# A graph layer with experts on one core: tighter edge slots and a reordered SyncE list in the first stage

## The chip, the cores and the metric

The kernel runs on one core of a Trainium2 chip. The metric is the device time of one execution in microseconds (us), lower is better. TensorE multiplies, VectorE, ScalarE and GpSimd compute on tiles of 128 partitions, SyncE only issues DMA transfers. Each engine works through its own list of instructions in order and waits on semaphores.

## The reference

There are N = 3125 nodes with D = 256 features and E = 50000 edges (`src`, `dst`). The edges are sorted by `dst`, and low node numbers have far more of them (`dst` is 3125 times the square of a uniform number). Cut to what matters:

```python
x_i = x[tgt]; x_j = x[src]                          # x is layer-normalised
h = relu(concatenate([x_i, x_j - x_i]) @ W1 + b1)   # 50000 x 512
out = segment_sum(h @ W2 + b2, tgt) / (deg + 1e-8)
x = x + out
# then: layernorm, a router that takes 2 of 8 experts, each expert
# gelu(xn @ W1[e] + b1[e]) @ W2[e] + b2[e], weighed and added to x
```

## The kernel before

**Splitting the product.** `feat @ W1` is P[dst] + Q[src], where Q = xn @ W1[256:] + b1 and P = xn @ (W1[:256] - W1[256:]). The hidden sum per node is multiplied by W2 only once per node.

**The Q stage** (the first block) walks over the NT = 25 tiles of 128 nodes. For tile t, TensorE transposes the normalised x (`turn`, L739), ScalarE copies it back (L696), TensorE multiplies (`product_q`, L746), VectorE adds b1 into `q_buf[t % 4]` (`keep_q`, L505), and SyncE stores that to `q_rows` in HBM (L405). `q_buf` has four parts, so `keep_q(t)` waits until the store of tile t-4 has landed (`s_qst`). Four PSUM banks hold the products, so TensorE can be up to four tiles ahead of `keep_q`. ScalarE normalises tile t+4 (L702). VectorE takes the layernorm statistics of whole groups of tiles (`statistics(k)`, L487 and L490), at the tiles given by `STATS_AT`: the last three groups are tiles 14 to 18, 19 to 23 and 24. ScalarE's `root(k)` (L692) follows and stands in its list ahead of later normalisations.

Between these, VectorE works out where each node tile's edges lie: `count_in_rows` (after `keep_q(4)`) feeds a small TensorE product (L770, behind the product of tile 6), which `find_ends` reads; then come `add_slots`, `find_tiles`, `find_blocks` (L598 to L613), which signals `s_index`. GpSimd then runs eight indirect gathers (L461) that fetch the src and dst of every slot from two copies in HBM, `src_blocks` and `dst_blocks`, and casts them (L464, L465). `first_table` (L623 to L634) uses them on VectorE at tile `SPREAD_AT`, and TensorE transposes the result two tiles later (L774, L777).

**Edge slots.** A slot is 128 consecutive edges which are handled for one node tile. Before, slots are whole blocks of 128 edges at multiples of 128 (EB = 391 of them), and a block that holds edges of two tiles takes a slot for each. So NS = 416, rounded up to 16.

**The edge stage** (the second block) processes NS slots. For each, GpSimd issues one indirect gather of 128 rows of `q_rows`, 2 KB each, into a ring of 16 (`gath`, L979). It may run until 16 slots ahead of the `seed` (L1146) or `add_z` (L1020) that frees the ring's place. TensorE expands P (L1285 to L1289), ScalarE takes the relu (L1158), VectorE its low part (L1025), TensorE sums into the tile (L1308, L1309). P itself is made in the same stage, in 46 half products between the first 368 slots.

**After it** come a stage over the 25 node tiles (W2, residual, layernorm, router) and one over 56 expert slots.

If the edges are unsorted, or the slots do not fit, a flag `unsorted` makes the kernel run the edge stage 25 times (`n_pass`).

Of the kernel before, what the change touches and what calls it, by code (L numbers as in the profile page):

```python
# [85 lines left out]
def build(nc, x, src, dst, g_w1, g_b1, g_w2, g_b2, gamma, beta, wr, br, f_w1, f_b1, f_w2, f_b2, out):  # L86
# [7 lines left out]
    NS = ceil_div(EB + NT - 1, UNROLL) * UNROLL  # L94
    SC = ceil_div(NS + 1, P)
# [26 lines left out]
    with ctx:  # L122
# [85 lines left out]
        start_i = whole("start_i", [P, 32], I32, a_ctx)  # L208
        first_i = whole("first_i", [P, 32], I32, a_ctx)
        last_i = whole("last_i", [P, 32], I32, a_ctx)  # L210
        first_f = whole("first_f", [P, 32], F32, a_ctx)
# [3 lines left out]
        nslot = whole("nslot", [P, 32], F32, a_ctx)  # L215
        shift = whole("shift", [P, 32], F32, a_ctx)
# [4 lines left out]
        eblk_i = whole("eblk_i", [P, SC], I32, a_ctx)  # L221
# [149 lines left out]
        SUMS_AT, SPREAD_AT = 6, 18  # L371
# [3 lines left out]
        with nc.Block(no_gpsimd_drain=True) as block:  # L375

            @block.sync
            def _(sp):
# [19 lines left out]
                for k, v in ((0, src), (1, dst)):  # L398
# [12 lines left out]
            def _(pool):  # L411
# [56 lines left out]
            def _(dve):  # L468
# [72 lines left out]
                def find_ends():  # L541
# [5 lines left out]
                    then(dve.tensor_copy(start_i[:, 0:NT], start_f[:, 0:NT]))  # L547
                    then(dve.tensor_scalar(last_f[:, 0:NT], start_f[:, 1:NT + 1], -1.0, 0.0, ALU.add, ALU.max))
                    now()

                    then(dve.tensor_scalar(first_i[:, 0:NT], start_i[:, 0:NT], 7, None, ALU.arith_shift_right))
# [3 lines left out]
                    then(dve.tensor_copy(first_f[:, 0:NT], first_i[:, 0:NT]))  # L555
                    now()

                    then(dve.tensor_scalar(first_f[:, 0:NT], first_f[:, 0:NT], float(EB - 1), None, ALU.min))
                    then(dve.tensor_copy(last_f[:, 0:NT], last_i[:, 0:NT]))
                    then(dve.memset(nslot[:, :], 0.0))  # L560
                    now()
                    then(dve.tensor_tensor(last_f[:, 0:NT], last_f[:, 0:NT], first_f[:, 0:NT], ALU.subtract))
                    now()

                    then(dve.tensor_scalar(nslot[:, 1:NT], last_f[:, 0:NT - 1], 0.0, 1.0, ALU.max, ALU.add))
# [13 lines left out]
                def find_tiles():  # L579

                    then(dve.tensor_tensor(shift[:, 0:NT], first_f[:, 0:NT], base[0][:, 0:NT], ALU.subtract))
                    then(dve.tensor_tensor(too_soon[:, 0:NT], first_ok[:, 0:NT], base[0][:, 0:NT], ALU.is_gt))
                    now()
                    then(dve.tensor_reduce(soonest[:, :], too_soon[:, READY:NT], AX.X, ALU.max))
# [12 lines left out]
                def find_blocks():  # L597
                    then(dve.tensor_tensor(esort[:, :], esort[:, :], slot_no[:], ALU.add))  # L598
# [4 lines left out]
                    then(dve.tensor_tensor(ttmp[:], slot_no[:], esort[:, :], ALU.subtract))  # L603
# [5 lines left out]
                    then(dve.tensor_scalar(esort[:, :], esort[:, :], float(EB), None, ALU.min))  # L609
                    now()  # L610
                    then(dve.tensor_copy(eblk_i[:, :], esort[:, :]))
# [321 lines left out]
        with nc.Block(no_gpsimd_drain=True) as block:  # L933
# [28 lines left out]
            def _(pool):  # L962
# [1051 lines left out]
```

## Time and profile before

| | |
|---|---|
| three runs | 938.30, 938.99, 938.96 us, median 938.96 |
| profiled execution, its own time | 938.75 us |
| its span, first to last instruction | 937.0 us (so 1.75 us lie around it) |
| mean granted TensorE clock | 0.98 of full |
| busy share TensorE, VectorE, ScalarE, GpSimd | 92%, 69%, 65%, 67% |
| Q stage | 0 to 69.8 us |
| edge stage | 70.9 to 607.5 us |
| node stage and experts | from 608 us |

The busy shares are averages over four stages with different limits. Matmul ends are modelled, so a busy TensorE isn't one at its peak. Which wait ends last in each stage is read from the order of time of the engines there.

### The profile page before, as it was taken

How to read it: one execution, taken by the hardware profiler on the slowest of the kernel's cores; microseconds unless marked ns; L12 is line 12 of the kernel's file. 1: busy time of each engine (PE TensorE's matmuls, PEld its weight loads, DVE VectorE, ACT ScalarE, POOL GpSimd, SP SyncE). 2: the span in 40 equal slices, each digit the busy share in tenths (PEclk: the TensorE clock that was granted, in tenths of full speed). 3: DMA queues.
4: the chain of work that ended last, by engine and by line, in shares of the span. 5: the costliest groups of instructions: out<-in, count | busy, mean ns of one | idle time of the engine just before them, and what ended most of it. 6: DMA issues, size and time to landing. Idle time of an engine off the chain costs nothing. (4 is left out here: it accounts for less than half of the span.)

```text
span 937.0 us, 17831 instructions
## 1 busy us (share of the span) xinstructions
PE 860.0 (92%) x4174; PEld 664.6 (71%) x4175; DVE 644.1 (69%) x1646; ACT 613.4 (65%) x1351; POOL 624.7 (67%) x633
## 2 busy tenths in 40 slices
PE   6898999999999999989999998899988999999997
PEld 3345666666666667666766665589856999999996
DVE  5846888888888788788888887767785343333332
ACT  4325888888888888888989988844444343443442
POOL 2227777777777777777777777389015577776774
PEclk9997999999999999999999999999979999999999
DMA  8347788787788878877888777547731244444443
GB/s 264 120 163 218 233 244 246 237 251 244 240 241 241 240 233 243 241 240 242 239 239 249 245 239 234 168 151 213 218 123 40 47 74 75 75 74 70 77 69 42
DMA packets 88193, 171.93 MB, mean 183 GB/s; under 512 B 13773, under 2 KB 53591, under 8 KB 88033
## 3 DMA queue, kind: packets, MB, share of 16 engines
q0 software_dynamic: 44336, 124.33, 48.0%
q1 hardware_dynamic: 42785, 45.26, 16.3%
q10 hardware_dynamic: 944, 0.92, 0.3%
q8 instruction: 45, 0.74, 0.3%
q14 instruction: 83, 0.68, 0.2%
HBM read 149.48 MB, written 21.37 MB: 182 GB/s over the span
## 5 line engine op out<-in xcount | busy, mean ns | idle before, releaser
L979 POOL DMA_INDIRECT gath<-q_rows,idx_t x416 | 399.7, 961 | 141.5 <-issue 96.9
L1025 DVE SCALAR_TENSOR_TENSOR h_lo<-bank,h_hi 128x512 fp32r<-128x512 f32 x334 | 224.8, 684 | 43.5 <-ACT h_hi L1158 41.1
L1158 ACT ACTIVATE h_hi<-bank 128x512 fp32r<-128x512 f32 x334 | 195.7, 597 | 38.4 <-DVE bank L1020 17.9
L1146 ACT ACTIVATE bank<-gath 128x512 f32<-128x512 f32 x293 | 176.9, 604 | 19.6 <-DMA gath<-q_rows,idx_t 17.2
L1308 PE MATMUL agg_ps<-h_hi,oh 128*128 128x512 f32 x416 | 165.8, 399 | 0.3 <-DVE h_lo L1025 0.3
L1309 PE MATMUL agg_ps<-h_lo,oh 128*128 128x512 f32 x416 | 165.4, 398 | 0.0
L1288 PE MATMUL bank<-p_hi,ohT 128*128 x293 | 127.8, 436 | 36.1 <-ACT bank L1146 33.8
L1877 POOL DMA_INDIRECT out<-y_out,sca_i x56 | 93.8, 1675 | 49.5 <-DMA out<-y_out,sca_i 17.5
L1930 ACT ACTIVATE actT<-bank,b1T 128x128 f32<-128x128 f32 x224 | 64.0, 368 | 84.8 <-PE bank L1964 84.8
L1288 PEld LDWEIGHTS bank<-p_hi,ohT 128*128 128x128 f32 x293 | 55.7, 190 | 88.9 <-issue 80.8
L1289 PE MATMUL bank<-p_lo,ohT 128*128 x293 | 116.3, 397 | 0.0
L1964 PE MATMUL bank<-tokT,fw_now 128*128 128x128 f32 x896 | 109.7, 276 | 0.1
L1910 DVE TENSOR_TENSOR y_out<-agg_ps,b2f 128x256 f32<-128x256 f32 x56 | 23.8, 425 | 125.1 <-PE agg_ps L1976 123.3
L1976 PE MATMUL agg_ps<-fw,actT 128*128 x448 | 105.9, 380 | 0.1
L1964 PEld LDWEIGHTS bank<-tokT,fw_now 128*128 128x128 f32 x896 | 105.0, 193 | 0.6 <-issue 0.5
L1308 PEld LDWEIGHTS agg_ps<-h_hi,oh 128*128 128x128 f32 x416 | 78.9, 190 | 27.6 <-issue 1.9
L1003 DVE TENSOR_SCALAR oh<-iota_row,rel_t 128x128 fp32r<-128x128 f32 x416 | 93.4, 298 | 4.4 <-issue 4.4
L1309 PEld LDWEIGHTS agg_ps<-h_lo,oh 128*128 128x128 f32 x416 | 78.9, 190 | 12.0
L1976 PEld LDWEIGHTS agg_ps<-fw,actT 128*128 128x128 f32 x448 | 80.9, 190 | 9.0 <-issue 0.3
L1013 DVE TENSOR_SCALAR ohT<-rows_sb,slot_no 128x512 fp32r<-128x512 bf16 x104 | 52.3, 504 | 34.1 <-PE bank L1289 27.6
L1449 POOL DMA_INDIRECT agg_all<-xm_rows,gat_i x56 | 58.4, 1044 | 19.8 <-issue 14.3
L1025 DVE SCALAR_TENSOR_TENSOR h_lo<-deg_ps,h_hi 128x512 fp32r<-128x512 f32 x82 | 56.1, 684 | 13.7 <-ACT h_hi L1158 13.1
(267 smaller groups left out, 1271.3 us busy)
## 6 DMA issues: line engine op xcount, KB each, us to landing
rows_sb<-rel_blocks SPq DMA_DIRECT2D x104, 128.0 KB, 4.3
fw<-in_L_ffn_W SPq DMA_DIRECT2D x16, 512.0 KB, 4.9
gath<-q_rows,idx_t POOLq DMA_INDIRECT x416, 4.3
q_rows<-q_buf SPq DMA_DIRECT2D x25, 256.0 KB, 2.5
out<-x_all SPq DMA_DIRECT2D x28, 128.0 KB, 3.2
x_all<-in_x SPq DMA_DIRECT2D x25, 128.0 KB, 2.5
xm_rows<-xt SPq DMA_DIRECT2D x25, 128.0 KB, 2.7
x_all<-in_x SPq DMA_DIRECT2D x2, 640.0 KB, 12.8
```

Of the source, the lines that this page charges most:

```text
L979: pool.indirect_dma_start(out=gath[:, j % RING, :], out_offset=None, in_=q_rows[:, :], in_offset=bass.IndirectOffsetOnAxis(ap=idx_t[:, j:j ...
L1003: ins = dve.tensor_scalar(oh[:, q % 4, k, :], iota_row[:], rel_t[:, bass.ds(local + k, 1)], None, ALU.is_equal)
L1025: dve.scalar_tensor_tensor(out=h_lo[:, j % LO_RING, :], in0=z_of(slot0, j), scalar=0.0, in1=h_hi[:, j % HI_RING, :].bitcast(F32), op0=ALU. ...
L1146: actv.activation(z_of(slot0, j), gath[:, j % RING, :], ACT.Copy).then_inc(s_seed, 1)
L1158: actv.activation(h_hi[:, j % HI_RING, :], z_of(slot0, j), ACT.Relu).then_inc(s_hi, 1)
L1288: pe.matmul(z, w, p_hi[:, tile, :], start=False, stop=True, skip_group_check=True)
L1289: pe.matmul(z, w, p_lo[:, tile, :], start=False, stop=True, skip_group_check=True).then_inc(s_exp_seeded, 1)
L1308: pe.matmul(agg_ps[:, par, :], w, h_hi[:, j % HI_RING, :], **more)
L1309: pe.matmul(agg_ps[:, par, :], w, h_lo[:, j % LO_RING, :], **more).then_inc(s_sum, 1)
L1877: pool.indirect_dma_start(out=out[:, :], out_offset=bass.IndirectOffsetOnAxis(ap=sca_i[:, i:i + 1], axis=0), in_=y_out[:, i % OUTS, :], in ...
L1964: ins = pe.matmul(bank[i % 2][:, h * P:(h + 1) * P], fw1_now[:, i % 2, k, h * P:(h + 1) * P], tokT[:, i % 2, k * P:(k + 1) * P], start=(k ...
L1976: ins = pe.matmul(agg_ps[:, i % 2, 0:D], actT[:, i % 2, k * P:(k + 1) * P], fw2[:, experts[i], k, :], start=(k == 0), stop=(k == KH - 1))
```

## The change

Three things change.

1. **Slots by edge, not by block.** A node tile's slots begin at its own first edge: `shift` becomes start minus 128 times the tile's first slot, a tile takes ceil(edges / 128) slots (at least 1), and the row gathers start at any edge (`edge_at`, an offset in elements of 4 bytes, where `eblk_i` was a block of 512 bytes). The first pass has NS = ceil4(391 + ceil(50/3)) = 408 slots. Further passes, for unsorted edges, still have NS_ALL = 416. A new comparison (`too_soon[:, NT]`) sets the flag for these if more than 408 slots are needed.
2. **SyncE's list of the Q stage.** The load of tiles 19 to 23, the load of the last tile (53 rows), the copies of src and dst, and the first half of W1 move from ahead of all stores of Q to behind the stores of tiles 0, 1, 2 and 3, and 4.
3. **`SPREAD_AT`** goes from 18 to 19, so `first_table` and what follows it come one tile later.

```diff
-    NS = ceil_div(EB + NT - 1, UNROLL) * UNROLL
-    SC = ceil_div(NS + 1, P)
+    NS = ceil_div(EB + ceil_div(2 * NT, 3), GROUP) * GROUP
+    NS_ALL = ceil_div(max(NS, EB), UNROLL) * UNROLL
+    SC = ceil_div(NS_ALL + 1, P)
...
-        SUMS_AT, SPREAD_AT = 6, 18
+        SUMS_AT, SPREAD_AT = 6, 19
...
-                for k in range(4, len(parts) - 1):
+                for k in range(4, len(parts) - 2):
                     load_x(k)
-                sp.dma_start(x_all[0:TAIL, NT - 1, :], x[(NT - 1) * P:N, :]).then_inc(s_x[-1], 16)
-
-                sp.dma_start(w1g[:, 0:KD, :], g_w1.rearrange("(k p) h -> p k h", p=P)[:, 0:KD, :]).then_inc(s_w[0], 16)
...
                     sp.dma_start(q_rows[t * P:(t + 1) * P, :], q_buf[:, t % Q_RING, :]).then_inc(s_qst[t % Q_RING], 16)
+                    if t == 0:
+                        load_x(len(parts) - 2)
+                    if t == 1:
+                        sp.dma_start(x_all[0:TAIL, NT - 1, :], x[(NT - 1) * P:N, :]).then_inc(s_x[-1], 16)
+                    if t == 2:
+                        copy_edges(0, src)
+                    if t == 3:
+                        copy_edges(1, dst)
+                    if t == 4:
+                        sp.dma_start(w1g[:, 0:KD, :], g_w1.rearrange("(k p) h -> p k h", p=P)[:, 0:KD, :]).then_inc(s_w[0], 16)
...
-                        pool.indirect_dma_start(out=rows_i[:, k, c, :], out_offset=None, in_=v[:, :],
-                                                in_offset=bass.IndirectOffsetOnAxis(ap=eblk_i[:, c:c + 1], axis=0)).then_inc(s_rows, 16)
+                        pool.indirect_dma_start(out=rows_i[:, k, c, :], out_offset=None, in_=v.rearrange("a (b o) -> (a b) o", o=1),
+                                                in_offset=bass.IndirectOffsetOnAxis(ap=edge_at[:, c:c + 1], axis=0)).then_inc(s_rows, 16)
...
-                    then(dve.tensor_tensor(shift[:, 0:NT], first_f[:, 0:NT], base[0][:, 0:NT], ALU.subtract))
+                    then(dve.scalar_tensor_tensor(out=shift[:, 0:NT], in0=base[0][:, 0:NT], scalar=float(-P), in1=start_f[:, 0:NT],
+                                                  op0=ALU.mult, op1=ALU.add))
+                    then(dve.tensor_scalar(too_soon[:, NT:NT + 1], base[0][:, NT:NT + 1], float(NS), None, ALU.is_gt))
...
+                        fetch(j)
 
                 for b in range(Q_RING):
                     pool.wait_ge(s_qst[b], 16 * len(range(b, NT, Q_RING)))
                 gathers(0)
                 n = pool.value_load(n_pass[0:1, 0:1], min_val=1, max_val=NT)
                 with pool.If(n > 1):
+                    pool.wait_ge(s_closed, after(0))
+                    for j in range(NS, NS_ALL):
+                        fetch(j)
```

In SyncE's list, from the loads of tiles 10 on, there stand before all the loads, then the copies, then the 25 stores:

```order
L381 DMA x_all<-in_x 128x4x256
L381 DMA x_all<-in_x 128x5x256 x2
L393 DMA x_all<-in_x 53x256
L395 DMA w1g<-in_L_gnn_W 128x2x512
L399 DMA src_blocks<-in_src 16x3125
L401 DMA src_blocks<-pad_i 1x176
L399 DMA dst_blocks<-in_dst 16x3125
L401 DMA dst_blocks<-pad_i 1x176
L405 DMA q_rows<-q_buf 128x512 x25
```

and now, from the load of tiles 14 to 18:

```order
L380 DMA x_all<-in_x 128x5x256
L403 DMA q_rows<-q_buf 128x512
L380 DMA x_all<-in_x 128x5x256
L403 DMA q_rows<-q_buf 128x512
L407 DMA x_all<-in_x 53x256
L403 DMA q_rows<-q_buf 128x512
L397 DMA src_blocks<-in_src 16x3125
L399 DMA src_blocks<-pad_i 1x176
L403 DMA q_rows<-q_buf 128x512
L397 DMA dst_blocks<-in_dst 16x3125
L399 DMA dst_blocks<-pad_i 1x176
L403 DMA q_rows<-q_buf 128x512
```

So one large transfer now stands between each two of the first stores of Q, and the first store is five places further forward.

In VectorE's list, `find_ends` after its first three instructions was

```order
L547 CAST start_i<-start_f 128x25
L548 TENSOR_SCALAR last_f<-start_f 128x25
L551 TENSOR_SCALAR first_i<-start_i 128x25
L552 CAST last_i<-last_f 128x25
L554 TENSOR_SCALAR last_i<-last_i 128x25
L555 CAST first_f<-first_i 128x25
L558 TENSOR_SCALAR first_f<-first_f 128x25
L559 CAST last_f<-last_i 128x25
L560 MEMSET nslot 128x32
L562 TENSOR_TENSOR last_f<-last_f,first_f 128x25
L565 TENSOR_SCALAR nslot<-last_f 128x24
```

and is now

```order
L555 MEMSET nslot 128x32
L556 SCALAR_TENSOR_TENSOR last_f<-start_f 128x25
L559 CAST last_i<-last_f 128x25
L561 TENSOR_SCALAR last_i<-last_i 128x25
L563 CAST last_f<-last_i 128x25
L565 TENSOR_SCALAR nslot<-last_f 128x25
```

Five instructions have gone, and the chain of steps that wait for each other is one shorter.

## Rows read from the trace of the kernel before

**Rows 1.** The page's costliest group: busy, mean ns of one, idle before it.

```profile
L979 POOL DMA_INDIRECT gath<-q_rows,idx_t x416 | 399.7, 961 | 141.5 <-issue 96.9
```

**Rows 2.** GpSimd's waits from 71 to 598 us: total, times, longest.

```profile
POOL gath L979 <- issue: 96.9, 318, 0.3
POOL gath L979 <- ACT bank L1146: 21.6, 71, 0.3
```

**Rows 3.** GpSimd in order of time: start, duration, idle before; first and last edge gathers.

```profile
70.98 0.97 POOL L979 DMA_INDIRECT gath<-q_rows,idx_t  x1 [14.98 <-DMA q_rows<-q_buf]
...
596.17 0.95 POOL L979 DMA_INDIRECT gath<-q_rows,idx_t  x1 [0.30 <-ACT bank L1146]
```

**Rows 4.** Busy time of each engine in a stretch in the middle of the edge stage.

```profile
200.00:300.00 100.00, 91.91 (x378) 67.52 (x376) 83.59 (x198) 84.58 (x165) 75.69 (x80) 1.00 0.79 243
```

**Rows 5.** VectorE in order of time, Q stage.

```profile
12.02 0.69 DVE L505 TENSOR_TENSOR q_buf<-agg_ps,b1g 128x512 f32<-128x512 f32 x1
...
15.07 0.69 DVE L505 TENSOR_TENSOR q_buf<-agg_ps,b1g 128x512 f32<-128x512 f32 x1 [0.80 <-PE agg_ps L746]
...
20.79 0.15 DVE L524 TENSOR_SCALAR cnt<-steepest 125x1 f32<-125x1 f32 x1
25.68 0.69 DVE L505 TENSOR_TENSOR q_buf<-agg_ps,b1g 128x512 f32<-128x512 f32 x1 [4.73 <-DMA q_rows<-q_buf]
...
28.36 0.69 DVE L505 TENSOR_TENSOR q_buf<-agg_ps,b1g 128x512 f32<-128x512 f32 x1 [0.64 <-DVE cnt L535]
...
31.09 0.66 DVE L505 TENSOR_TENSOR q_buf<-bank,b1g 128x512 f32<-128x512 f32 x1
...
33.68 0.18 DVE L565 TENSOR_SCALAR nslot<-last_f 128x24 f32<-128x24 f32 x1
...
42.95 0.45 DVE L490 BATCH_NORM_AGGREGATE mv<-stats 128x2 f32<-128x6 f32 x5
...
56.10 0.88 DVE L633 TENSOR_SCALAR gath<-dst_rows,ttmp 128x128 f32<-128x128 f32 x4 [2.39 <-POOL src_rows L465]
```

**Rows 6.** TensorE in order of time, Q stage.

```profile
22.83 1.88 PE L746 MATMUL bank<-w1g,x_all 128*128 128x512 f32 x4
27.84 0.41 PE L770 MATMUL deg_ps<-cnt,ones_mat 125*128 125x32 f32 x2 [3.12 <-DVEq L537]
...
28.34 3.44 PE L746 MATMUL bank<-w1g,x_all 128*128 128x512 f32 x4
...
44.28 0.44 PE L739 MATMUL bank<-ident,xn_buf 128*128 128x128 f32 x2 [0.74 <-ACT xn_buf L702]
...
57.89 0.60 PE L774 MATMUL deg_ps<-ident,src_rows 128*128 128x128 f32 x4
```

**Rows 7.** Busy time, granted clock and DMA share of two microseconds of the Q stage.

```profile
25.00:26.00 1.00, 0.00 (x0) 0.00 (x0) 0.32 (x1) 0.00 (x0) 0.00 (x0) 1.00 0.08 29
29.00:30.00 1.00, 1.00 (x3) 0.48 (x2) 1.00 (x5) 0.00 (x0) 0.00 (x0) 0.50 0.12 45
```

**Rows 8.** SyncE's issues in order of time, Q stage.

```profile
5.19 5.71 SPq L381 DMA_DIRECT2D x_all<-in_x  x3
...
13.82 2.82 SPq L395 DMA_DIRECT2D w1g<-in_L_gnn_W  x1
...
18.94 40.62 SPq L405 DMA_DIRECT2D q_rows<-q_buf  x21
```

**Rows 9.** The first store of q_rows: time from issue to landing.

```profile
DMA to landing us min/median/max: 6.6/6.6/6.6
```

**Rows 10.** All loads of x_all up to 30 us: time from issue to landing.

```profile
DMA to landing us min/median/max: 2.5/9.4/12.9
```

**Rows 11.** GpSimd in order of time, row gathers and casts of the Q stage.

```profile
41.11 1.02 POOL L461 DMA_INDIRECT rows_i<-src_blocks,eblk_i  x1 [21.18 <-DVEq L613]
...
54.83 0.61 POOL L464 CAST dst_rows<-rows_i 128x512 f32<-128x512 int32 x1 [3.00 <-DMA rows_i<-dst_blocks,eblk_i]
55.38 0.61 POOL L465 CAST src_rows<-rows_i 128x512 f32<-128x512 int32 x1
```

More of the change, by code:

```diff
@@ L215, in build @@
         nslot = whole("nslot", [P, 32], F32, a_ctx)
+        past_last = whole("past_last", [P, SC], F32, a_ctx)
         shift = whole("shift", [P, 32], F32, a_ctx)
@@ L220, in build @@
         esort = whole("esort", [P, SC], F32, a_ctx)
-        eblk_i = whole("eblk_i", [P, SC], I32, a_ctx)
+        edge_at = whole("edge_at", [P, SC], I32, a_ctx)
         rows_i = whole("rows_i", [P, 2, SC, P], I32, a_ctx)
@@ L597, in find_blocks @@
                 def find_blocks():
-                    then(dve.tensor_tensor(esort[:, :], esort[:, :], slot_no[:], ALU.add))
+                    then(dve.scalar_tensor_tensor(out=esort[:, :], in0=slot_no[:], scalar=float(P), in1=esort[:, :], op0=ALU.mult, op1=ALU.add))
                     now()
@@ L601, in find_blocks @@
                     now()
-                    then(dve.tensor_tensor(ttmp[:], slot_no[:], esort[:, :], ALU.subtract))
+                    then(dve.scalar_tensor_tensor(out=ttmp[:], in0=slot_no[:], scalar=float(P), in1=esort[:, :], op0=ALU.mult, op1=ALU.subtract))
                     now()
@@ L626, in first_table @@
                     now()
[L627 removed]
+                    then(dve.tensor_tensor(ttab[:], ttab[:], past_last[:, :], ALU.max))
                     now()
@@ L872, in build @@
         s_settled = {e.engine: sem(f"s_settled{k}") for k, e in enumerate((nc.gpsimd, nc.scalar, nc.tensor, nc.vector))}
-        TRIPS = NS // UNROLL
-        assert NS % UNROLL == 0 and SC * P > NS and UNROLL % RING == 0 and RING % Z_RING == 0
+        TRIPS = NS_ALL // UNROLL
+        assert NS_ALL - NS < RING and NS % GROUP == 0 and UNROLL % RING == 0 and RING % Z_RING == 0
         passes, further, branched = {}, {}, {}
+        no_added, no_seeded = (n(NS_ALL) - n(NS) for n in (added_before, seeded_before))
+        no_groups = (NS_ALL - NS) // GROUP
+        unused = {nc.vector.engine.name: ((s_z, no_added), (s_lo, NS_ALL - NS), (s_oh, no_groups)),
+                  nc.scalar.engine.name: ((s_seed, no_seeded), (s_hi, NS_ALL - NS), (s_ohT, no_groups)),
+                  nc.tensor.engine.name: ((s_exp_added, no_added), (s_exp_seeded, no_seeded), (s_sum, NS_ALL - NS), (s_ohT_ps, no_groups))}
         def branch_to_further(eng, one_pass):
@@ L889, in further_passes @@
             with nc.body(f"further_{name}", parent=branched[name], valid_engines=[eng.engine]):
+                for s, n in unused[name]:
+                    eng.sem_inc(s, n)
                 with eng.Fori(1, passes[name]) as p:
@@ L962, in _, with fetch @@
             def _(pool):
+                def fetch(j):
+                    pool.indirect_dma_start(
+                        out=gath[:, j % RING, :], out_offset=None, in_=q_rows[:, :],
+                        in_offset=bass.IndirectOffsetOnAxis(ap=idx_t[:, j:j + 1], axis=0)).then_inc(s_g[j % RING], 16)
                 def gathers(p):
@@ L966, in gathers @@
                         settle(pool)
-                    base = held(pool, p * NS)
-                    added, seeded = held(pool, p * added_before(NS)), held(pool, p * seeded_before(NS))
-                    for j in range(NS):
+                    added, seeded = held(pool, p * added_before(NS_ALL)), held(pool, p * seeded_before(NS_ALL))
+                    for j in range(NS if isinstance(p, int) else NS_ALL):
                         if is_added(j):
@@ L978, in gathers @@
                             settle(pool)
-                        pool.indirect_dma_start(
-                            out=gath[:, j % RING, :], out_offset=None, in_=q_rows[:, :],
-                            in_offset=bass.IndirectOffsetOnAxis(ap=idx_t[:, j:j + 1], axis=0)).then_inc(s_g[j % RING], 16)
+                        fetch(j)
                 for b in range(Q_RING):
@@ L1047, in table @@
                     dve.wait_ge(s_closed, after(p - 1))
+                    for j in range(NS, NS_ALL):
+                        dve.wait_ge(s_g[j % RING], 16 * (NS_ALL // RING))
                     step(dve.tensor_scalar(ttmp[:], tsort[:], pass_no[:], -1.0, ALU.subtract, ALU.mult))
```

36 lines of the change are left out of this document (14 added, 22 removed).

## The prediction

> **What bounds the kernel now.** I read the page first. Its costliest group is the gather of the edge stage, 416 times with 399.7 us of busy time [rows 1]. The busy shares would point at TensorE, which is busy 91.9 of 100 us in that stage, against GpSimd's 75.7 [rows 4]. The waits say otherwise. In the whole stage GpSimd's gaps ahead of gathers are never over 0.3 us, most of them with no releaser (318 times), and those put down to ScalarE are just as short (71 times) [rows 2]. In order of time, one gather takes 0.95 us with 0.30 us ahead of it, and the last looks like any other [rows 3]. An engine that never waits for longer than its own gap between instructions is the one that paces. From the first gather to the last it is 596.17 - 70.98 = 525.19 us for 415 steps, 1.2655 us each. TensorE's work of a slot fits into that and its gaps cost nothing.
>
> In the Q stage I read the order of time on VectorE, TensorE and SyncE. VectorE is done at 20.94, then stands still for 4.73 us until the store of `q_buf`'s first part has landed [rows 5]. SyncE issued that store only at 18.94, behind all loads and copies, although VectorE had filled it at 12.02 + 0.69 = 12.7 [rows 5, 8]. Then `count_in_rows` is late, and TensorE, whose product L770 needs it, idles 3.12 us. It comes back at half clock: the product at 28.34 takes 3.44 us instead of 1.88 [rows 6], and the granted clock of that stretch is 0.50, that is 1.2 GHz after 3 us without work [rows 7]. From there VectorE is the late one: it is almost never idle up to the end of the statistics of tiles 19 to 23 at 42.95 + 0.45 = 43.40, and 0.88 us behind them, through ScalarE's root, TensorE's turn begins at 44.28 after a wait of 0.74 [rows 5, 6]. Afterwards TensorE paces: from 44.28 to the transposes at 57.89 there are seven tiles, 1.94 us each [rows 6]. The edge stage begins when the last store of Q has landed [rows 3], so what TensorE gains in this stage, all later work gains.
>
> **The slots.** 416 become 408. All slots are executed, filled or not, and GpSimd issues one gather for each. So 8 x 1.2655 = **10.1 us** go. Taken away are also eight slots of the other engines, which lay beside. What follows the last gather is the same pipeline of eight slots, so nothing comes back there. Bounds: 9.6 us, if the eight cost only the bare 0.95 + 0.30 (10.0) and the drain is a little less well filled, to 10.5.
>
> Does the new placement need no more than 408? I worked it out from the reference's own draw of `dst`: the sum over the 25 tiles of ceil(edges / 128) is 403. So there is one pass, and five slots are empty.
>
> **SyncE's list.** The first store now goes out at 12.7, since only the load of tiles 14 to 18 stands ahead, and SyncE had issued three loads by 10.9 [rows 8]. Under the load of this stretch the first store took 6.6 us to land [rows 9], so it lands at 19.3. VectorE needs it at 20.95, when the product of tile 4 is done too (that of tile 5 has ended by 22.83). The wait is gone. Then `count_in_rows` ends 2.04 us later (25.68 to 28.36 less the 0.64 of waiting), at 23.0, and TensorE, which is free at 24.72, does not wait.
>
> How much is that? From TensorE's side: 3.12 of idle time, 3.44 - 1.88 = 1.56 at half clock, and some 0.2 for the two small operations between 27.84 and 28.34: 4.9 us. From VectorE's side, which decides until 43.40: the stretch from 25.68 to 43.40 is 17.72 us and now begins at 20.95. It loses one step of `find_ends` (0.2 us, a chain step is as long as the row at 33.68), and perhaps the 0.64 ahead of 28.36, if that was the second store and not the step named. It ends at 37.8 to 38.5, and the turn begins 0.88 later, at 38.7 to 39.4 instead of 44.28: a gain of 4.9 to 5.6. TensorE by itself could not be there before 24.72 + 0.25 + 7 x 1.94 = 38.55, so 5.7 is the ceiling. I take **5.2 us**.
>
> Two more stores are now behind a large transfer. Store 1 is issued at 15.07 + 0.69 = 15.8, even if the load ahead of it blocks SyncE for 2.82 us as the one at 13.82 did [rows 5, 8]. With 6.6 us it lands at 22.4; VectorE wants it at 23.0. Store 2, behind the 53-row load, goes out at 18.9 at the latest and lands at 25.5; VectorE wants it 31.09 - 28.36 = 2.73 after 23.0, at 25.7. Both are in time, with 0.6 and 0.2 to spare. Later stores have one more microsecond of slack per tile. The first half of W1 and the edge copies are wanted some 34 us or later, over 10 us after their issue, which is within 12.9, the longest landing of any load here [rows 10].
>
> **The table one tile later.** GpSimd's row gathers and casts take from 41.11 to 55.38 + 0.61 = 55.99 [rows 11], and now begin 5.2 earlier: done at 50.8. VectorE had reached `first_table` 2.39 us before 56.10 [rows 5], so now, a tile later, at 53.71 - 5.2 + 1.94 = 50.45; it waits some 0.4 us, which four PSUM banks cover, and is done at 51.8. TensorE wants it at 57.89 - 5.2 + 1.94 = 54.6: 2.8 us in hand. So **0**.
>
> **Sum.** 938.75 - 10.1 - 5.2 = 923.45 for the profiled execution; the median of the runs is 0.2 above it, so 923.6.
>
> **Rivals.**
> - *The stall is only moved.* Store 1 or 2 lands later than 6.6 us after its issue, and every microsecond of it delays VectorE, which decides there. At 12.9 us, the longest landing [rows 10], store 0 alone lands at 25.6, as late as now. Then only the slots count: 928.6. Half of it lost gives 926. For it: margins of 0.6 and 0.2 us. Against: there is less ahead of each store than there was ahead of the one that took 6.6. Chance 0.12.
> - *The 53-row load holds up store 2.* Between 25 and 26 us, with the first store not there yet, only 8% of the DMA engines' time was used, about one engine of 16, at 29 GB/s [rows 7]. So one engine was behind. If the load of 53 rows is what it worked on, then now, with that load right ahead of store 2, its 53 KB take 53 / 29 = 1.8 us more: store 2 lands at 27.3 instead of 25.5, VectorE and all behind it are 1.6 us later, 925.2. Against: the row doesn't say whose bytes these were. Chance 0.1. The Trainium skill ("DMA: Bandwidth & Descriptors", section on why a DMA increments its semaphore by 16, on how many engines it runs on) speaks for this rival: a transfer's partition count is divided among the largest number of engines up to 16 that divides it, and 53 is prime, so it is one.
> - *Slower: row gathers that begin at any edge.* The eight gathers now start at multiples of 4 bytes, not 512, and no row here shows such a start. A slower landing counts once: even 12.9 us instead of the 3.0 of waiting [rows 10, 11] puts the table 9.9 later, less 2.8 in hand, 7 us: 930.6. Only if each took GpSimd longer would it turn: past 2.8 + 15.3 + 1.9 = 20 us in all, 2.5 us for each of eight on top of the present 1.25. At 4 us on top each it would be 938.75 - 15.3 + 29.2 = 952.7. Against: gathers of 2 KB and of 512 bytes a row both cost 0.95 to 1.02 [rows 3, 11], so the cost is not in the bytes. Chance 0.03 for slower, 0.02 for the dearer landing.
> - *The flag is set,* and there are 25 passes of some 516 us: 403 against 408 speaks against it. Chance 0.01.
> - *The 408 don't save their full step,* since another engine would pace: nothing in [rows 2] says so. Taken into the range.
>
> The Trainium skill (same page, on how a descriptor splits into AXI transactions) says that a descriptor which does not start on 256 bytes takes a further transaction: 3 for 2 here. If that made each row gather's 3.0 us of landing half longer, the last would land 1.5 us later, inside the 2.8, and the sum would stay. No row of before can show it.
>
> **The numbers.** Forecast 0.7, with its own range 921.8 to 925.2 (slots 9.6 to 10.5, Q stage 3.9 to 5.7, and 0.35 for the spread of runs). Store 2 held up 0.1, moved stall 0.12, dear gathers 0.05, flag 0.01, a larger gain 0.02. The range for 8 in 10 takes in the held store and half of the moved stall: 921.5 to 927. Under 0.2% (1.9 us) this measurement can't tell a difference. Faster than that 0.95, same 0.01, slower 0.04.
>
> **What would show it.** 408 gathers with a step of 1.265; VectorE's keep of tile 4 near 21 us without a wait for `q_rows`; no idle time ahead of the small product near 24.7, and a clock of 1.00 there; the transposes of the table near 54.6; the first edge gather near 65.8, the last near 581. A wait of VectorE for `q_rows` at the keeps of tiles 5 or 6 means the moved stall. A wait of TensorE ahead of the transposes means the row gathers.

## The result and the profile after

The changed kernel takes **922.94 us**, median of 4 runs (922.78 to 924.52). The kernel before took 938.98 us in the same comparison (4 runs, 938.30 to 939.11). The ratio is 0.9832, with a 95% interval of 0.9814 to 0.9850: it is 1.7% faster, clear of the spread of the runs. The profiled execution took 922.85 us, its span is 921.0 us, against 938.75 and 937.0 before.

The costliest group on the page, then GpSimd's waits from 66 to 581 us (total, times, longest), answer to [rows 1, 2]:

```profile
L974 POOL DMA_INDIRECT gath<-q_rows,idx_t x408 | 390.7, 958 | 138.8 <-issue 99.4
```

```profile
POOL gath L974 <- issue: 99.4, 326, 0.3
POOL gath L974 <- ACT bank L1163: 20.1, 66, 0.3
```

GpSimd in order of time: first and last row gather of the Q stage, the casts, first and last edge gather, and the first instruction of the node stage:

```profile
36.16 1.02 POOL L469 DMA_INDIRECT rows_i<-src_blocks,edge_at  x1 [16.25 <-DVEq L615]
...
45.99 0.94 POOL L469 DMA_INDIRECT rows_i<-dst_blocks,edge_at  x1 [0.30 <-issue]
50.18 0.61 POOL L472 CAST dst_rows<-rows_i 128x512 f32<-128x512 int32 x1 [3.25 <-DMA rows_i<-dst_blocks,edge_at]
50.74 0.61 POOL L473 CAST src_rows<-rows_i 128x512 f32<-128x512 int32 x1
66.09 0.97 POOL L974 DMA_INDIRECT gath<-q_rows,idx_t  x1 [14.74 <-POOLq L374]
...
579.99 0.95 POOL L974 DMA_INDIRECT gath<-q_rows,idx_t  x1 [0.30 <-issue]
...
594.83 0.18 POOL L1720 IOTA eidx<- 128x56 f32 x1 [13.89 <-POOLq L943]
```

GpSimd still never waits longer than 0.3 us in the edge stage, so by its waits it still paces. There are 408 gathers with a mean step of (579.99 - 66.09) / 407 = 1.2627 us. The first comes 4.89 us earlier than before.

VectorE in the Q stage, in order of time (start, duration, idle before):

```profile
21.23 0.69 DVE L513 TENSOR_TENSOR q_buf<-agg_ps,b1g 128x512 f32<-128x512 f32 x1
...
23.91 0.69 DVE L513 TENSOR_TENSOR q_buf<-agg_ps,b1g 128x512 f32<-128x512 f32 x1 [0.64 <-DVE cnt L543]
...
26.64 0.66 DVE L513 TENSOR_TENSOR q_buf<-bank,b1g 128x512 f32<-128x512 f32 x1
...
28.66 0.18 DVE L565 TENSOR_SCALAR nslot<-last_f 128x25 f32<-128x25 f32 x1
...
38.06 0.45 DVE L498 BATCH_NORM_AGGREGATE mv<-stats 128x2 f32<-128x6 f32 x5
...
51.60 0.87 DVE L636 TENSOR_SCALAR gath<-dst_rows,ttmp 128x128 f32<-128x128 f32 x4
```

The keep of tile 4 (21.23) has no wait any more where 4.73 us stood. TensorE in the same stage:

```profile
24.90 0.31 PE L773 MATMUL deg_ps<-cnt,ones_mat 125*128 125x32 f32 x2
25.04 0.42 PE L742 MATMUL bank<-ident,xn_buf 128*128 128x128 f32 x2
25.30 1.88 PE L749 MATMUL bank<-w1g,x_all 128*128 128x512 f32 x4
...
39.39 0.44 PE L742 MATMUL bank<-ident,xn_buf 128*128 128x128 f32 x2 [0.58 <-ACT xn_buf L705]
...
54.94 0.60 PE L777 MATMUL deg_ps<-ident,src_rows 128*128 128x128 f32 x4
```

The small product at 24.90 follows without idle time, and the product behind it takes 1.88 us, not 3.44. The granted clock there is 1.00, the 2.4 GHz level; in this row it is the number behind the five engines' busy times and ahead of the DMA share and the GB/s:

```profile
25.00:26.00 1.00, 1.00 (x7) 0.68 (x6) 1.00 (x4) 0.38 (x1) 0.00 (x0) 1.00 0.96 357
```

SyncE's issues in order of time. Seven of them that stood ahead of the first store (three loads, two copies and their two pads) now stand behind stores, not five as the text on the change says:

```profile
12.89 0.35 SPq L403 DMA_DIRECT2D q_rows<-q_buf  x1
13.29 0.43 SPq L380 DMA_DIRECT2D x_all<-in_x  x1
16.13 0.34 SPq L403 DMA_DIRECT2D q_rows<-q_buf  x1
16.52 0.29 SPq L407 DMA_DIRECT2D x_all<-in_x  x1
18.07 0.33 SPq L403 DMA_DIRECT2D q_rows<-q_buf  x1
```

The trace gives these three stores 6.7, 5.7 and 6.2 us from issue to landing. So they landed at 19.6, 21.8 and 24.3, and VectorE's keeps of tiles 4, 5 and 6 began at 21.23, 23.91 and 26.64.

**Where the 16.0 us of span came from.** The first edge gather is 4.89 us earlier. From it to the node stage it took 610.23 - 70.98 = 539.25 us before and takes 594.83 - 66.09 = 528.74 now, 10.51 less. The rest, from the node stage to the end, took 326.77 and takes 326.17, 0.60 less, which nothing in the change explains. (610.23 is the row of GpSimd's same instruction before:)

```profile
610.23 0.18 POOL L1703 IOTA eidx<- 128x56 f32 x1 [13.12 <-POOLq L933]
```

### The profile page after: what moved, and what is told of

It reads as the page before. It is cut to its first block and busy times, and to the rows that moved or that the text cites. A ratio compares the mean times of both kernels' runs of the same rounds, so it can differ in the third digit from the quotient of the medians.

```text
span 921.0 us, 17640 instructions
## 1 busy us (share of the span) xinstructions
PE 846.7 (92%) x4140; PEld 657.9 (71%) x4141; DVE 636.7 (69%) x1624; ACT 604.3 (66%) x1336; POOL 616.4 (67%) x625
## 5 line engine op out<-in xcount | busy, mean ns | idle before, releaser
L974 POOL DMA_INDIRECT gath<-q_rows,idx_t x408 | 390.7, 958 | 138.8 <-issue 99.4
L1040 DVE SCALAR_TENSOR_TENSOR h_lo<-bank,h_hi 128x512 fp32r<-128x512 f32 x327 | 220.7, 685 | 44.8 <-ACT h_hi L1175 42.3
L1175 ACT ACTIVATE h_hi<-bank 128x512 fp32r<-128x512 f32 x327 | 191.1, 597 | 37.8 <-DVE bank L1035 17.1
L1163 ACT ACTIVATE bank<-gath 128x512 f32<-128x512 f32 x286 | 173.0, 605 | 18.8 <-DMA gath<-q_rows,idx_t 14.9
L1325 PE MATMUL agg_ps<-h_hi,oh 128*128 128x512 f32 x408 | 162.1, 397 | 0.2 <-DVE h_lo L1040 0.2
L1326 PE MATMUL agg_ps<-h_lo,oh 128*128 128x512 f32 x408 | 161.5, 396 | 0.0
L1305 PE MATMUL bank<-p_hi,ohT 128*128 x286 | 124.1, 434 | 39.1 <-ACT bank L1163 36.0
L1306 PE MATMUL bank<-p_lo,ohT 128*128 x286 | 113.7, 397 | 0.0
L1326 PEld LDWEIGHTS agg_ps<-h_lo,oh 128*128 128x128 f32 x408 | 77.0, 189 | 12.1
## 6 DMA issues: line engine op xcount, KB each, us to landing
x_all<-in_x SPq DMA_DIRECT2D x2, 640.0 KB, 10.5
```

The lines of the kernel that those rows point to most:

```text
L974: pool.indirect_dma_start(out=gath[:, j % RING, :], out_offset=None, in_=q_rows[:, :], in_offset=bass.IndirectOffsetOnAxis(ap=idx_t[:, j:j ...
L1040: dve.scalar_tensor_tensor(out=h_lo[:, j % LO_RING, :], in0=z_of(slot0, j), scalar=0.0, in1=h_hi[:, j % HI_RING, :].bitcast(F32), op0=ALU. ...
L1163: actv.activation(z_of(slot0, j), gath[:, j % RING, :], ACT.Copy).then_inc(s_seed, 1)
L1175: actv.activation(h_hi[:, j % HI_RING, :], z_of(slot0, j), ACT.Relu).then_inc(s_hi, 1)
L1305: pe.matmul(z, w, p_hi[:, tile, :], start=False, stop=True, skip_group_check=True)
L1306: pe.matmul(z, w, p_lo[:, tile, :], start=False, stop=True, skip_group_check=True).then_inc(s_exp_seeded, 1)
```

## The experiments

All kernels below share one addition that has nothing to do with the question: each tile number and each count of turns that an engine reads into a register is put through a maximum with 0. The control kernels show what it costs.

```diff
-            return vals
+            return [eng.snap(smax(v, 0)) for v in vals]
```

### The parts of the change, first job

**The changed kernel itself:**

> The changed kernel with one register operation more behind every loaded tile number and turn count (a maximum with 0), which all kernels of this study carry. If GpSimd paces the edge stage, one operation more on TensorE's and ScalarE's sequencers per slot lies beside its 1.263 us step: 922.9 as the changed kernel, within 1. If TensorE paced, 408 slots at some 0.05 us each would show: 940 or so.

**The list alone**, that is the kernel before with the new SyncE list (point 2 of the change) and nothing else:

> The kernel before with SyncE's new list alone (416 slots, table at tile 18). Theory (the store's landing was the stall, the rest of the stage follows): 4.9 us less than before, less the one chain step that only the new placement saves: 4.7, so 934.3. The first edge gather starts near 66.3 and there are 416 gathers. Rival (the stall is moved, or most of the 16 us came from the slots): within 1.9 of 939.

**The slots alone**, the changed kernel with SyncE's old list (its lines are left out here) and the table back at tile 18:

```diff
-        SUMS_AT, SPREAD_AT = 6, 19
+        SUMS_AT, SPREAD_AT = 6, 18
```

> The changed kernel with SyncE's list and the table's place of before. Theory (each slot costs GpSimd's step): 8 x 1.2655 = 10.1 less than before, plus some 0.2 for the shorter chain: 928.7. TensorE's idle 3.1 us ahead of its small product and the half clock behind it are there again. Rival (slots beyond the pace are cheap, for instance because empty slots run faster): 934 or more.

**The 53-row load alone**, the kernel before with one line moved:

```diff
-                sp.dma_start(x_all[0:TAIL, NT - 1, :], x[(NT - 1) * P:N, :]).then_inc(s_x[-1], 16)
...
                     sp.dma_start(q_rows[t * P:(t + 1) * P, :], q_buf[:, t % Q_RING, :]).then_inc(s_qst[t % Q_RING], 16)
+                    if t == 1:
+                        sp.dma_start(x_all[0:TAIL, NT - 1, :], x[(NT - 1) * P:N, :]).then_inc(s_x[-1], 16)
```

> The kernel before with only the 53-row load moved, to behind the store of tile 1. If that load kept a single DMA engine busy and so held the first store's landing, the store now lands 1.8 us earlier or more and VectorE's wait of 4.73 us falls to some 2.9 or less. If the queue in front of the store is what counts (SyncE gets to it only after all loads), the wait falls by the load's own issue slot of 2.8 us at most. If the bytes ahead alone count (53 of some 2200 KB still to move), it falls by 0.3 or less.

This job ran on a chip where all of these kernels took 1127 to 1148 us, the one before too (1141.47, median of 14). In the four traces from it the edge stage is interrupted every eight slots. Its times can't judge a forecast made for 939 us, so the expected times above are neither met nor missed here. Its Q stage ran as usual and can be read. Measured: changed kernel 1131.10 us, ratio 0.9908 (0.9874 to 0.9942); list alone 1140.67, ratio 1.0001 (0.9978 to 1.0024); slots alone 1132.72, ratio 0.9934 (0.9913 to 0.9956); 53-row load alone 1147.95 in its one run. GpSimd in the changed kernel on that chip:

```profile
216.19 0.95 POOL L976 DMA_INDIRECT gath<-q_rows,idx_t  x1 [0.30 <-issue]
221.98 0.94 POOL L976 DMA_INDIRECT gath<-q_rows,idx_t  x1 [4.84 <-DVE bank L1037]
...
230.74 0.95 POOL L976 DMA_INDIRECT gath<-q_rows,idx_t  x1 [0.30 <-issue]
235.63 0.94 POOL L976 DMA_INDIRECT gath<-q_rows,idx_t  x1 [3.95 <-DVE bank L1037]
```

Where something other than GpSimd stops the stage for mostly 3.8 to 4.9 us every eight slots, the list alone is worth nothing measurable in the end, although its first edge gather came at 66.31 us, as early as the changed kernel's 66.29 (slots alone 70.48).

What the Q stage shows. VectorE of the list alone, then VectorE of the 53-row load alone, then its SyncE and TensorE:

```profile
21.00 0.69 DVE L515 TENSOR_TENSOR q_buf<-agg_ps,b1g 128x512 f32<-128x512 f32 x1
```

```profile
24.21 0.69 DVE L507 TENSOR_TENSOR q_buf<-agg_ps,b1g 128x512 f32<-128x512 f32 x1 [3.00 <-DMA q_rows<-q_buf]
```

```profile
11.29 3.80 SPq L395 DMA_DIRECT2D w1g<-in_L_gnn_W  x1
...
17.50 0.83 SPq L405 DMA_DIRECT2D q_rows<-q_buf  x2
```

```profile
42.82 0.69 PE L741 MATMUL bank<-ident,xn_buf 128*128 128x128 f32 x2 [2.32 <-DVE q_buf L507]
43.30 3.31 PE L748 MATMUL bank<-w1g,x_all 128*128 128x512 f32 x4
```

The list alone takes the wait away whole, so the stall came from the list and from nothing in the slots. Moving the 53-row load alone brings the store out at 17.50, against 18.84 in the slots-alone kernel on the same chip, and VectorE's wait is 3.00 us against 4.03 there; the landing still takes 6.6 us from the issue. So 53 KB are worth 1.3 to 1.4 us of the store's time, nearly all of it by an earlier issue. The busy share of the DMA engines changed too. With the 53-row load ahead of the store there are two microseconds at 6 to 10% and 25 to 37 GB/s around the landing ([rows 7], and the same in both traces of the slots alone). With it moved, the two microseconds ahead of the landing are at 28 and 29%; the second of them:

```profile
23.00:24.00 1.00, 1.00 (x6) 0.52 (x5) 0.00 (x0) 0.70 (x2) 0.00 (x0) 1.00 0.28 108
```

And nothing of the gain arrived. The turn of tile 16 came 1.46 us earlier than in the kernel before (42.82 against 44.28), but TensorE had waited 2.32 us for it and came back at 3.31 us a product, and the first edge gather was at 71.15 us. More on that under "Idle time or half clock?".

### The parts of the change, second job

> SyncE's new list alone, as before. Where the edge stage runs at GpSimd's step of 1.26 us per slot, the theory expects 934.3 (4.7 less than before), with the first edge gather near 66.3. Rival, after the run at 1141: what the Q stage gains is given back in the edge stage, so within 1.9 of the kernel before even though the first gather starts 4.7 us earlier.

> The new slots alone, as before. Theory: 928.7, that is 10.1 and some 0.2 less than before, 408 gathers at a step of 1.265 us from 70.9 on. Rival: the gains of list and slots don't add up to the 16.0 of the whole change, by more than 1.5 us.

Measured on a chip where the kernel before took 939.40 us (7 runs, 938.16 to 940.76): list alone **933.28**, ratio 0.9934 (0.9917 to 0.9950); slots alone **926.80**, ratio 0.9864 (0.9847 to 0.9880). The profiled execution of the list alone took 1400.10 us at a mean granted clock of 0.56, where its other four took 932.49 to 934.16, so no time is compared with it. Slots alone, its VectorE and then its TensorE:

```profile
25.79 0.69 DVE L505 TENSOR_TENSOR q_buf<-agg_ps,b1g 128x512 f32<-128x512 f32 x1 [4.52 <-DMA q_rows<-q_buf]
```

```profile
27.95 0.41 PE L765 MATMUL deg_ps<-cnt,ones_mat 125*128 125x32 f32 x2 [2.91 <-DVEq L537]
...
28.45 1.88 PE L741 MATMUL bank<-w1g,x_all 128*128 128x512 f32 x4
...
43.96 0.44 PE L734 MATMUL bank<-ident,xn_buf 128*128 128x128 f32 x2 [1.88 <-ACT xn_buf L697]
```

The wait is all there. The half clock behind it, which was expected too, is not: the product takes 1.88 us. The first edge gather is at 70.66 us, and from it to the node stage it takes 528.92 us, 10.33 less than before. The list met its expectation. The slots came out 1.9 us below theirs, a little more than the interval; in the trace 0.3 of it is ahead of the first gather and 1.05 behind the edge stage, where the slots change nothing. So each part brings its gain by itself. By the medians the two add up to 6.1 + 12.6 = 18.7 us, more than the 16.0 of the whole; each interval is some 1.6 us to either side, so that is no evidence of an interaction. The traces add up. Ahead of the first gather the list alone gives 70.98 - 66.31 = 4.67 us (first job) and the slots alone 0.32, together 4.99 against the 4.89 of the whole; behind it the slots alone give 10.33 against 10.51.

### Does TensorE pace the edge stage?

The changed kernel without the product with the low part of P, one of two products of every expansion; the output lacks that part.

```diff
                     if is_added(j):
-                        pe.matmul(z, w, p_hi[:, tile, :], start=True, stop=False)
-                        pe.matmul(z, w, p_lo[:, tile, :], start=False, stop=True).then_inc(s_exp_added, 1)
+                        pe.matmul(z, w, p_hi[:, tile, :], start=True, stop=True).then_inc(s_exp_added, 1)
```

> The changed kernel without the product with the low part of P in each slot (one of five matmuls of 512 columns per slot; the sum is taken with the high part only). That takes 0.23 us per slot from TensorE, 95 us over the stage. Theory (GpSimd paces): the step of the gathers stays 1.26 us and the time falls by less than 2 us, to 921 to 923. Rival (TensorE, busy 92% of the stage, paces): the stage is some 95 us shorter, 830 or so.

One run: 926.16 us. The same stretch as in [rows 4], in this kernel:

```profile
200.00:300.00 100.00, 83.24 (x301) 52.73 (x300) 84.77 (x201) 84.84 (x166) 75.88 (x80) 0.98 0.81 241
```

TensorE is busy 83.2 of 100 us instead of 91.9, GpSimd the same as ever (75.9), and the step from gather to gather is 1.2644 us, no shorter. The time isn't shorter either, though 921 to 923 had been expected: it is 3 us longer than the changed kernel, in this one run, 1.2 of it ahead of the first gather, 0.8 in the edge stage and 1.3 behind it. The rival is out: the engine with the highest busy share isn't the bound.

What the edge stage looks like when TensorE does pace can be seen in the execution of 1400.10 us above. From 300 to 400 us TensorE is busy for all 100 us, at a granted clock of 0.56, and GpSimd waits 4.9 us ahead of every eighth gather.

The run without the low part also shows who is waited for. ScalarE's `seed` needs a gather's rows. Its waits for them between 100 and 560 us (total, times, longest), in the changed kernel and then in this one:

```profile
ACT bank L1163 <- DMA gath<-q_rows,idx_t: 9.8, 13, 1.7
```

```profile
ACT bank L1165 <- DMA gath<-q_rows,idx_t: 25.4, 38, 1.5
```

With less work on TensorE the other engines come to wait for the gathers more often, and GpSimd's own waits stay at 0.3 us. No run made ScalarE or VectorE lighter, or a gather cheaper, so against these two as the bound only the waits speak.

### Fewer slots still

404 slots instead of 408; the reload of x is moved forward by one group of four slots, so that the last one still fits. The graph needs 403.

```diff
-    NS = ceil_div(EB + ceil_div(2 * NT, 3), GROUP) * GROUP
+    NS = ceil_div(EB + ceil_div(NT, 2), GROUP) * GROUP
```

> The changed kernel with 404 slots in the first pass (403 are filled), and SyncE's reloads of x one group of slots earlier in its list, so that the last is still issued. Theory (each slot one step): 4 x 1.263 = 5.1 less than the changed kernel, 917.9. Rival (empty slots at the end are cheap, as their work is hidden in the drain): 922 to 923.

And with the statistics of tiles 19 to 23 one tile earlier as well, in another job:

```diff
-        STATS_AT = {3: 1, 4: 3, 5: 6, 6: 11, 7: 15}
+        STATS_AT = {3: 1, 4: 3, 5: 6, 6: 10, 7: 15}
```

> The changed kernel with 404 slots in place of 408, and the statistics of tiles 19 to 23 one tile earlier. Theory: GpSimd paces the edge stage, and VectorE decides in the Q stage until these statistics. 404 slots alone gave 919.9 us. The earlier statistics take away the wait of 0.58 us ahead of TensorE's turn of tile 16, so the first gather comes at 65.5 and the time is 919.3. Rival: the statistics then delay VectorE's chain to the table by their 2.3 us, TensorE waits ahead of the transposes, and the time is 920 to 921.

Measured: 404 slots **919.89 us**, ratio 0.9791 (0.9773 to 0.9809); with the earlier statistics **919.57 us**, ratio 0.9785 (0.9769 to 0.9801). Both ratios are some 0.4% below the changed kernel's 0.9830 and 0.9832, about 4 us. The two kernels of one job, 0.9785 and 0.9830, have intervals that don't meet, so it is a gain. The intervals don't exclude the 5 us of four slots; the traces do. From first gather to node stage the 404 take 525.29 us, only 3.45 less than the 408's 528.74, where 4 x 1.2627 = 5.05 was due. The gathers did save it: first to last took 508.40 us, 5.50 less. So did the sums: from the first gather to the end of the last sum it is 520.93 us against 526.19, 5.26 less. What is missing went after the last sum. TensorE and ScalarE at the end of the edge stage, with 404 slots and the earlier statistics:

```profile
587.50 0.40 PE L1328 MATMUL agg_ps<-h_lo,oh 128*128 128x512 f32 x1
```

```profile
586.77 0.60 ACT L1190 ACTIVATE agg_ps<-zero_r 128x512 f32 x1
590.33 0.60 ACT L1187 ACTIVATE agg_all<-agg_ps  x1 [2.96 <-issue]
```

and ScalarE of the changed kernel there, whose last sum ended at 592.28:

```profile
592.61 0.60 ACT L1185 ACTIVATE agg_all<-agg_ps  x1 [2.26 <-PE agg_ps L1326]
```

With 408, the last tile is closed 0.33 us after the last sum. With 404 it is 590.33 - 587.90 = 2.43 us (2.44 in the other 404 kernel), and ScalarE's gap ahead of it has no releaser. In the code ScalarE reads 17 tile numbers into registers ahead of every sixteenth slot. The last such reading is ahead of slot 400: eight slots before the end of 408, four before the end of 404, where nothing is left to hide it. That this reading is the gap is argued from the code, not shown; part of it may be the added maxima, 17 of them.

The earlier statistics did what they were meant to: TensorE's wait ahead of the turn of tile 16 is gone, and the first gather comes at 65.65 us instead of 66.36. The edge stage behind it took 1.3 us more than in the other 404 kernel, so the two times can't be told apart. Those 1.3 us lie ahead of the end of the last sum (522.25 us behind the first gather, against 520.93), and their cause is open.

### Idle time or half clock?

The wait for the store came with 3.12 us of idle time on TensorE and 1.56 us at half clock. This kernel is the one before, with three idle products that keep TensorE busy during the wait; they write to a bank that isn't read.

```diff
                     if t == SUMS_AT:
+                        keep_awake(pe, 3)
                         pe.wait_ge(s_cnt, 2)
```

> The kernel before, with three dummy products of TensorE ahead of its wait for the counts. It separates the two parts of the price that the stall had for TensorE: the waiting (which stays, VectorE still waits 4.7 us for the store) and the half clock behind it (1.56 us). My theory: VectorE decides until the statistics at 43.4, so the product at 28.34 takes 1.88 us instead of 3.44, but TensorE's turn of tile 16 stays near 44.3 and the time stays within 0.5 us of 938.9. Rival: TensorE's half clock is itself on the path, then TensorE's turn begins 1.5 us earlier and the time is 937.4.

And, in the same job, the changed kernel again:

> The changed kernel, with two register maxima on GpSimd as in the other experiment kernels. If those cost nothing, 922.9 us as for the changed kernel itself, first gather near 66.1 and last near 580. The comparisons with the other three kernels here are made against this run.

Measured, with the kernel before at 938.74 us (15 runs, 936.71 to 941.16): awake **939.46 us**, ratio 1.0005 (0.9990 to 1.0020), no difference; changed kernel **923.87 us**, ratio 0.9830 (0.9809 to 0.9851), the first result again, so the register maxima cost nothing that shows. TensorE of the awake kernel:

```profile
28.02 0.41 PE L772 MATMUL deg_ps<-cnt,ones_mat 125*128 125x32 f32 x2 [0.31 <-DVEq L538]
...
28.51 1.88 PE L747 MATMUL bank<-w1g,x_all 128*128 128x512 f32 x4
...
44.44 0.44 PE L740 MATMUL bank<-ident,xn_buf 128*128 128x128 f32 x2 [2.31 <-ACT xn_buf L703]
44.72 3.17 PE L747 MATMUL bank<-w1g,x_all 128*128 128x512 f32 x4
...
59.75 0.60 PE L776 MATMUL deg_ps<-ident,src_rows 128*128 128x128 f32 x4
```

The product behind the stall takes 1.88 us as hoped, and the turn of tile 16 is at 44.44, where it was at 44.28. TensorE has run ahead and now waits there, 2.31 us instead of 0.74. So in this stretch VectorE decides, as the prediction had it. Behind this wait the half clock stands now: granted clock 0.59 and 0.50 from 45 to 47 us, a product of 3.17 us, and the transposes at 59.75, 15.31 behind the turn instead of 13.61. The first edge gather is at 72.83 us, 1.85 later than before, though the measured ratio shows no loss; its interval reaches up to 1.9 us. The trace is of one execution out of ten, which took 937.26 to 942.20 us; whether all of them had the half clock at that place isn't known.

The 53-row kernel of the first job went the same way: a wait of 2.32 us at the turn of tile 16, a product of 3.31 us, and 42.82 to 58.07 = 15.25 us to the transposes instead of 13.61. In this later stretch TensorE paces, so here the half clock costs its full 1.6 to 1.7 us, and it took back all that the earlier store had given.

How long TensorE waits doesn't tell by itself whether the clock falls. The slots-alone kernel was traced twice. The second job's trace, above, has 2.91 us of idle time ahead of the small product and full clock behind it. The first job's has less idle time and the half clock:

```profile
27.77 0.63 PE L765 MATMUL deg_ps<-cnt,ones_mat 125*128 125x32 f32 x2 [2.42 <-DVEq L537]
...
28.67 2.97 PE L741 MATMUL bank<-w1g,x_all 128*128 128x512 f32 x4
```

The pair also answers the question of this section once more. The turn of tile 16 was at 43.77 us with the half clock and at 43.96 without: up to there it cost nothing, as VectorE decides.

### Row gathers at any edge

The changed kernel, with the starts of the row gathers rounded down to multiples of 128 edges; it handles other edges than it should.

```diff
+                    then(dve.tensor_scalar(edge_at[:, :], edge_at[:, :], 7, 7, ALU.arith_shift_right, ALU.arith_shift_left))
```

> The changed kernel, with the starts of the row gathers rounded down to multiples of 128 edges, so that each is a multiple of 512 bytes again; the edges that it then handles are not those of its slots. All else stays. If starts at any edge cost something in the landing, GpSimd's wait ahead of the casts goes from 3.25 back to 3.00 us; if the 0.25 is scatter it stays at 3.1 to 3.4. My theory: nothing hangs on it, since the table is wanted later, and the time is 922.9 either way. Rival (each unaligned gather costs GpSimd time as well): first cast 2 us earlier, and if that were on the path 921.

Measured: 923.88 us, against 923.87 of the changed kernel in the same job. GpSimd:

```profile
50.25 0.61 POOL L473 CAST dst_rows<-rows_i 128x512 f32<-128x512 int32 x1 [3.23 <-DMA rows_i<-dst_blocks,edge_at]
```

The wait is 3.23 us with aligned starts and 3.25 without, in the changed kernel's first trace and in that of the same job. The starts cost nothing in the landing, and the eight gathers take GpSimd the same time.

## Why the prediction was right

**What bounds the kernel.** Right. That TensorE isn't the bound is shown: with half of its expansion products left out nothing gets shorter. That GpSimd is rests on its waits, never over 0.3 us, and on ScalarE's waits for its gathers, which grew when TensorE got lighter; with fewer slots the stage gets shorter by GpSimd's step for each.

**The slots, 10.1 us.** Measured 10.51 in the first trace and 10.33 in the slots-alone kernel, at and inside the upper bound of 10.5. The eight steps are 8 x 1.2627 = 10.1. The remainder is mostly one gather of 1.77 us in the trace of before, 0.82 over the usual, that after doesn't have:

```profile
73.50 1.77 POOL L979 DMA_INDIRECT gath<-q_rows,idx_t  x1 [0.30 <-issue]
```

It isn't scatter. The third gather of the edge stage takes 1.76 to 1.78 us in all five traces with 416 slots (before, awake, 53-row load, list alone twice) and 0.95 us in those with the new slots. The prediction had no term for it, and its cause is open.

The drain behind the last gather took 14.84 us instead of 14.06, but that isn't a price of the slots: the awake kernel, with its 416, has 14.92 and gathers that are 0.62 us shorter in all. From the first gather to the node stage it is 539.25 and 539.49 us with 416 slots and 528.74, 528.92 and 528.94 with 408. So "nothing comes back there" held for these eight slots. It didn't hold for the four that the 404 kernels leave out.

**SyncE's list, 5.2 us.** Measured 4.89, at the lower end of 4.9 to 5.6. Its terms one by one:
- The keep of tile 4 without a wait, forecast 20.95, came at 21.23: VectorE was 0.3 later from the second tile on (15.41 against 15.07).
- The 0.64 us ahead of the next keep. I left open whether it was the second store or the step named. It stayed at 0.64 with the store landed at 21.8, 1.4 us before VectorE could have used it (23.91 - 0.64 = 23.27): it is the step. This took the forecast from its upper half to its lower.
- `find_ends` and what follows lost more than the one step of 0.2. From the keep at 21.23 to the end of the statistics at 38.51 it took 17.28 us, against 17.72: 0.44. `find_ends` itself got 0.57 shorter, as the steps that are gone or lighter held two or three instructions each and lasted some 0.3 us (from 32.25 to 33.46 there are four). 0.13 of it came back behind it, where a comparison and a table are new. All of this 0.44 belongs to the new slots, not to the list.
- Sum: 4.45 + 0.44 = 4.89 at the statistics, and the turn of tile 16 followed 0.88 us behind, as before, at 39.39. The first edge gather came 26.70 us behind that turn in the kernel before (70.98 - 44.28), in the changed one (66.09 - 39.39) and in the slots-alone one (70.66 - 43.96). So what the turn gains, the first gather gains.

**The table one tile later, 0.** Right. GpSimd was done with the casts at 51.35, forecast 50.8, VectorE didn't wait for it (forecast: 0.4), and TensorE found the table done 54.94 - 52.47 = 2.5 us ahead.

**The moved stall.** Not seen. The margins of stores 1 and 2 had been put at 0.6 and 0.2 us; they were 1.4 and 2.4. For store 1 the issue at 16.13 was even 0.3 later than forecast, with VectorE; it landed after 5.7 us instead of 6.6. For store 2 the issue was 0.8 earlier: I had let each load block SyncE for 2.82 us, as before, but with the stores between them the loads took SyncE 0.43 and 0.29 us. And VectorE wanted it 0.9 later, since the 0.64 us ahead of the keep of tile 5 had been left out of the 25.7. That both margins were forecast too small and not too large is luck: the three landings differ by up to 1.0 us, more than the margins that had been counted on.

**The 53-row load.** Store 2, right behind it, landed after 6.2 us, between the 6.7 and 5.7 of the other two, so the 1.8 us of the rival didn't come. That this load had a part in the old stall is shown: moved by itself it gave 1.3 to 1.4 us. That this was the one busy engine of [rows 7] isn't shown, though such a row is gone ahead of the landing once the load is moved. The size of the gain agrees with it, but would also with a load that only keeps SyncE, and the unchanged 6.6 us from issue to landing speak for that. The Trainium skill ("DMA: Bandwidth & Descriptors", on why a DMA increments its semaphore by 16) gives such a transfer a single engine. By it and the 29 GB/s of the row, 1.8 us of one engine's queue would go, an estimate; the measured 1.3 to 1.4 lie near it and don't prove it.

**Row gathers at any edge.** The two kernels that differ in nothing else show 3.25 and 3.23 us: no cost. The Trainium skill ("DMA: Bandwidth & Descriptors", on how a descriptor splits into AXI transactions) has three transactions for such a row instead of two; of the 1.5 us that half as long again would be, this measurement shows nothing.

**The sum.** 923.6 forecast, 922.94 measured. The 0.6 is a slot term 0.4 too small, a list term 0.3 too large, and 0.6 us after the edge stage that belong to no step. Part of the hit is luck, as these three partly cancel. The forecast's own range, 921.8 to 925.2, also doesn't come out of its terms: 10.5 + 5.7 and 9.6 + 3.9, with 0.35 to either side, give 922.2 to 925.6. The measured time lies in both.

## What to carry to other kernels

Find the pacing engine by its waits and not by its busy share: in this edge stage GpSimd at 76% with no wait over 0.3 us set the pace, TensorE at 92% did not, and taking work from it gave nothing. In an in-order DMA list, a store that frees a buffer belongs ahead of every load that is needed later; large loads one behind the other also keep the issuing engine itself. A gain at the head of a chain counts only up to the next engine that decides: relieving the engine that merely waits there moves its wait to the next place, and a clock drop there can cost more than one at the old place, as it did in the 53-row kernel.

## What the runs showed of the hardware that was not expected

- SyncE's issue of one load took 2.8 us in a row of large loads [rows 8] and 0.29 to 0.43 us between stores.
- TensorE's granted clock stayed full behind waits of 1.88 and 2.91 us and was half behind waits of 2.31, 2.32, 2.42 and 3.12 us (products of 3.17, 3.31, 2.97 and 3.44 us instead of 1.88). The same kernel showed both at the same place, so the length of the wait alone doesn't decide it.
- The third gather of the edge stage took 1.76 to 1.78 us in every trace with 416 slots and 0.95 us in those with the new slots. The cause is open.
- VectorE's step from its own last counting instruction to the keep behind it had 0.64 or 0.65 us of idle time in every trace but the one of 1400 us, whether a store had been late or not. What it waits for beyond that instruction is open.
- On one chip the edge stage of all four kernels traced there stood still every eight slots, mostly for 3.8 to 4.9 us and once for 5.9 (mean step 1.73 to 1.75 us instead of 1.26), with the Q stage and the node stage as fast as elsewhere. The rhythm of eight isn't that chip's: GpSimd's waits have it too in the execution of 1400 us, on another chip, where TensorE was busy throughout. What held the stage up there is open.
